# Selective scan: unit pairs of neighbouring channels, one 512 KB replication per pair, and another order of the y sums

## What is computed

```
xs = jnp.stack([x0, x1, x0[..., ::-1], x1[..., ::-1]], axis=1)        # 4 directions k
delta = jax.nn.softplus(dts + dt_projs_bias[None, :, :, None])
def step(h, inp):
    u_t, d_t, B_t, C_t = inp
    h = jnp.exp(d_t[..., None] * A) * h + (d_t * u_t)[..., None] * B_t[:, :, None, :]
    y = jnp.einsum('bkdn,bkn->bkd', h, C_t)
    return (h, y)
ym = ys[:, 0:2] + ys[:, 2:4][..., ::-1]
y = ym[:, 0] + ym[:, 1].reshape(B, D, W, H).transpose(0, 1, 3, 2).reshape(B, D, L)
```

## Time and profile before

| | |
|---|---|
| runs (3) | median 5447.71 us, 5444.3 to 5461.19 us |
| profiled execution, its own time | 5458.66 us |
| its span, first to last instruction | 5456.5 us |
| the scan's part of it | about 2756 to 5366 us |
| busy in the span: PE, DVE, ACT, POOL | 4633.9, 4354.1, 3138.7, 4137.1 us |

### The profile page before, as it was taken

The page is one execution under the profiler, slowest core; times in us unless marked ns, Lnnn a source line. Parts: engine busy times, 40 slices in busy tenths (PEclk is TensorE's granted clock), DMA queues, the critical chain, the costliest instruction groups (busy, mean ns, idle before and its releaser), DMA issues. The chain is left out here.

```text
span 5456.5 us, 68516 instructions
## 1 busy us (share of the span) xinstructions
PE 4633.9 (85%) x15210; PEld 2099.0 (38%) x15210; DVE 4354.1 (80%) x3524; ACT 3138.7 (58%) x6582; POOL 4137.1 (76%) x1958
## 2 busy tenths in 40 slices
PE   7998887956999999964978888888888888888887
PEld 2332554623666666642522222222222222222222
DVE  4776445452599999997969999999988999999995
ACT  6885555621111111101367788887878778888876
POOL 2454545532589898987869999899998999999993
PEclk9998999977999999977979999999998999999998
DMA  2000101067678787844067777777776777777773
GB/s 52 1 1 15 55 22 51 27 195 203 134 141 151 140 153 140 152 73 99 0 152 186 183 194 183 182 188 177 188 188 170 187 185 187 182 190 179 191 184 98
DMA packets 385380, 733.14 MB, mean 134 GB/s; under 512 B 77948, under 2 KB 119080, under 8 KB 370920
## 3 DMA queue, kind: packets, MB, share of 16 engines
q1 hardware_dynamic: 385128, 730.30, 56.8%
HBM read 594.31 MB, written 82.32 MB: 124 GB/s over the span
## 5 line engine op out<-in xcount | busy, mean ns | idle before, releaser
L2208 POOL TENSOR_TENSOR l_hc<-l_h,l_c_rep 128x1024 f32<-128x1024 f32 x768 | 1805.8, 2364 | 212.3 <-DVE l_h L2279 206.0
L1400 POOL TENSOR_TENSOR l2b_prod<-l2b_v,l2b_attn 128x1568 f32<-128x1568 f32 x276 | 937.9, 3458 | 232.0 <-ACT l2b_attn L1361 117.3
L2279 DVE TENSOR_TENSOR_SCAN l_h<-l_p,l_h,l_bu 128x1024 f32<-128x1024 f32 x448 | 1030.9, 2337 | 71.8 <-ACT l_bu L2116 70.7
L1964 PE MATMUL l_p<-l_stacked,l_pick 96*128 96x512 f32 x1536 | 656.2, 509 | 302.1 <-DVE l_h L2279 301.6
L2263 DVE TENSOR_TENSOR l_bu<-l_du_rep,l_p 128x1024 f32<-128x1024 f32 x512 | 616.5, 1204 | 133.9 <-DMA l_du_rep<-du_scratch 125.1
L1448 DVE TENSOR_REDUCE l2b_osum<-l2b_prod 128x32 f32<-128x1568 f32 x384 | 665.7, 1780 | 63.3 <-POOL l2b_prod L1400 59.5
L2197 POOL TENSOR_TENSOR l_pool_bu<-l_du_rep,l_b_sb 128x1024 f32<-128x1024 f32 x256 | 605.2, 2364 | 40.3 <-DMA l_du_rep<-du_scratch 40.3
L1964 PEld LDWEIGHTS l_p<-l_stacked,l_pick 96*128 96x128 f32 x1536 | 253.1, 196 | 989.2 <-DVE l_h L2279 815.1
L1973 PE MATMUL l_p<-l_hc,l_y_pick 128*32 128x512 f32 x3072 | 582.3, 646 | 3.7 <-POOL l_hc L2208 3.7
L1353 ACT ACTIVATE l2b_logits<-l2b_conv,l2b_this_b 98x512 f32<-98x512 f32 x96 | 66.2, 689 | 861.0 <-PE l2b_conv L1318 861.0
L2279 DVE TENSOR_TENSOR_SCAN l_h<-l_p,l_h,l_pool_bu 128x1024 f32<-128x1024 f32 x224 | 524.7, 2343 | 3.8 <-ACT l_pool_bu L2116 3.5
(11 more groups left out here) (269 smaller groups left out, 9066.2 us busy)
## 6 DMA issues: line engine op xcount, KB each, us to landing
l_du_rep<-du_scratch SPq DMA_DIRECT2D x1536, 256.0 KB, 5.2
l2b_img_high<-qkv_scratch SPq DMA_DIRECT2D x192, 306.2 KB, 5.7
l2b_img_low<-qkv_scratch SPq DMA_DIRECT2D x192, 306.2 KB, 9.5
l_stacked<-l_parts SPq DMA_DIRECT2D x512, 96.0 KB, 2.3
l2b_v<-v_scratch SPq DMA_DIRECT2D x192, 152.0 KB, 6.4
qkv_scratch<-l2a_strip SPq DMA_DIRECT2D x32, 840.0 KB, 5.2
du_scratch<-l_du SPq DMA_DIRECT2D x128, 192.0 KB, 2.1
l_w_raw<-L_w_sed SPq DMA_DIRECT2D x32, 576.0 KB, 3.7
```

Source lines behind the costliest of these rows:

```text
L1400: return eng.tensor_tensor(dst.rearrange("q x (dy dx) -> q x dy dx", dx=WIN), window, attn_half[:, :, unit % 2].rearrange("q x (dy dx) -> ...
L1964: pe.matmul(p_da[p % 2][:, e, :], pick[:, GRP[i] % (Q // DL), :], stacked[:, par, GRP[i] * DL // Q, :], start=True, stop=True).then_inc(s_ ...
L2208: pool.tensor_tensor(hc[:, slot:slot + 2, :], h[:, 2 * p:2 * p + 2, :], c_rep[:, par, :].unsqueeze(1).to_broadcast([128, 2, N]), ALU.mult) ...
L2279: dve.tensor_tensor_scan(flat(h[:, 2 * p:2 * p + 2, :]), flat(p_da[p % 2]), flat(of), state, ALU.mult, ALU.add).then_inc(s_h, 1)
```

## The change

A unit is now one channel parity: of 16 neighbouring channels the even ones are one unit and the odd ones the other, and the two make a pair. Two neighbouring rows of `du_scratch` lie behind each other in DRAM, so the du of a partition's two units is one run of 4 KB, where it was two runs of 2 KB. Each pair is replicated by one DMA of 512 KB where there were two of 256 KB, the ring has four slots of a pair in place of eight of a unit, and each product waits for one semaphore in place of two. SP replicates pair 0 of the next step right after the store of du, ahead of `restack`.

The y sums change their sets: the three units of a triple come from three pairs (the even units of pairs 0 to 2, then the odd ones, the same for pairs 3 to 5), where they were three units in a row. On PE the third triple and the fourth stand together ahead of the third pair's `replicate`; `low_mm` moves ahead of the fourth pair's `replicate`; `c_mm` moves behind the second triple. On ACT `turn_x` moves ahead of `low`. The constants `pick`, `y_pick` and `a_logs` are permuted to fit. DVE and POOL keep their order.

```diff
-    RING = 8
+    RING = 4
-    GRP = [(i % YT) * YJ + i // YT for i in range(G)]
+    GRP = [2 * (SETS * (p % YT) + p // YT) + e for p in range(PAIRS) for e in range(2)]
-        du_rep = sb("l3_du_rep", [128, RING, N])
+        du_rep = sb("l3_du_rep", [128, RING, 2, N])
...
-                src = du_d[par, GRP[i] * DL:(GRP[i] + 1) * DL]
-                src = bass.AP(src.tensor, src.offset, [[0, S], [N, DL], [1, N]])
-                sp_.dma_start(du_rep[:, ring_at(par, i)], src).then_inc(s_dur[ring_at(par, i)], 16)
+                first = GRP[2 * p] // 2 * (2 * DL)
+                src = du_d[par, first:first + 2 * DL]
+                src = bass.AP(src.tensor, src.offset, [[0, S], [2 * N, DL], [1, 2 * N]])
+                sp_.dma_start(du_rep[:, ring_at(par, p)].rearrange("q e n -> q (e n)"), src).then_inc(s_dur[ring_at(par, p)], 16)
...
             def step(n, par, more):
-                for i in range(RING, G):
-                    replicate_du(n, par, i)
+                for p in range(RING, PAIRS):
+                    replicate_du(n, par, p)
                 if more:
                     store_du(n + 1, 1 - par)
+                    replicate_du(n + 1, 1 - par, 0)
                     sp_.wait_ge(s_rep, G * n)
                     sp_.nop(nofuse=True)
                     restack(n + 1, 1 - par)
-                    for i in range(RING):
-                        replicate_du(n + 1, 1 - par, i)
+                    for p in range(1, RING):
+                        replicate_du(n + 1, 1 - par, p)
...
             def y_triple(n, t, par):
-                pe.wait_ge(s_hc, PAIRS * n + LAST_PAIR[t] + 1 + HC0)
+                first, e = YT * (t // 2), t % 2
+                pe.wait_ge(s_hc, PAIRS * n + first + YT + HC0)
...
-                                   hc[:, hc_at(par, i // 2) + i % 2, :], start=(t == 0), stop=False)
+                                   hc[:, hc_at(par, first + q) + e, :], start=(t == 0), stop=False)
...
                 if before:
                     y_triple(n - 1, 2, 1 - par)
+                    y_triple(n - 1, 3, 1 - par)
                 replicate(n, k, 2, par)
                 if before:
-                    y_triple(n - 1, 3, 1 - par)
                     y_whole(n - 1, *before)
+                if n1:
+                    low_mm(n + 1)
                 replicate(n, k, 3, par)
                 if n1:
-                    low_mm(n + 1)
                     b_mm(n + 1, 1 - par, *n1)
...
                 y_triple(n, 0, par)
                 replicate(n, k, 5, par)
+                y_triple(n, 1, par)
                 if n1:
                     c_mm(n + 1, *n1, n2)
-                y_triple(n, 1, par)
...
-                if n1:
-                    low(n + 1)
-                decays(n, k, c, 3)
-                if n1:
-                    b_copy(n + 1, 1 - par)
                 if k == 0:
                     if not isinstance(c, int):
                         turn_x(b, c + 2)
...
+                if n1:
+                    low(n + 1)
+                decays(n, k, c, 3)
+                if n1:
+                    b_copy(n + 1, 1 - par)
                 decays(n, k, c, 4)
...
-                triple = (2 * (freed % PAIRS) + 1) // YT
+                triple = 2 * (freed % PAIRS // YT) + 1
```

More of the change, by code:

```diff
@@ L1710, in selective_scan @@
     TRIPLES = G // YT
-    LAST_PAIR = [(YT * t + YT - 1) // 2 for t in range(TRIPLES)]
+    SETS = PAIRS // YT
     HCP = 4
-    RING = 8
+    RING = 4
     POOL_PAIRS = (2, 5)
@@ L1824, in all_steps, with ring_at, ring_count @@
             return run
[L1826 to L1832, removed]
+        def ring_at(par, p):
+            return (PAIRS * par + p) % RING
+        def ring_count(n, par, p):
+            return 16 * (2 * PAIRS // RING * (n - par) // 2 + (PAIRS * par + p) // RING) + 16
         def hc_at(par, p):
@@ L1876, in store_du, with replicate_du @@
                 sp_.dma_start(du_d[par], du[:]).then_inc(s_dus, 16)
-            def replicate_du(n, par, i):
-                if i == 0:
+            def replicate_du(n, par, p):
+                if p == 0:
                     sp_.wait_ge(s_dus, 16 * (n + 1) + DUS0)
                     sp_.nop(nofuse=True)
-                user, step_of = (i - RING) % G // 2, (i - RING) // G
+                user, step_of = (p - RING) % PAIRS, (p - RING) // PAIRS
                 if user in POOL_PAIRS:
@@ L1900, in step @@
                     restack(n + 1, 1 - par)
-                    for i in range(RING):
-                        replicate_du(n + 1, 1 - par, i)
+                    for p in range(1, RING):
+                        replicate_du(n + 1, 1 - par, p)
             store_du(0, 0)
+            replicate_du(0, 0, 0)
             restack(0, 0)
-            for i in range(RING):
-                replicate_du(0, 0, i)
+            for p in range(1, RING):
+                replicate_du(0, 0, p)
             step(0, 0, True)
@@ L1971, in y_triple @@
                 for q in range(YT):
-                    i = YT * t + q
                     mm = pe.matmul(p_y[q * 32:(q + 1) * 32, :], y_pick[:, t, :],
-                                   hc[:, hc_at(par, i // 2) + i % 2, :], start=(t == 0), stop=False)
+                                   hc[:, hc_at(par, first + q) + e, :], start=(t == 0), stop=False)
                 mm.then_inc(s_ymm, 1)
@@ L2189, in times_b @@
                     pool.nop(nofuse=True)
-                for e in range(2):
-                    pool.wait_ge(s_dur[ring_at(par, 2 * p + e)], ring_count(n, par, 2 * p + e))
-                    pool.nop(nofuse=True)
+                pool.wait_ge(s_dur[ring_at(par, p)], ring_count(n, par, p))
+                pool.nop(nofuse=True)
                 before = POOL_PAIRS[at - 1] + 1 if at else POOL_PAIRS[-1] + 1 - PAIRS
@@ L2195, in times_b @@
                     pool.wait_ge(s_h, PAIRS * n + before + H0)
-                slot = ring_at(par, 2 * p)
-                pool.tensor_tensor(pool_bu[:], du_rep[:, slot:slot + 2, :], b_sb[:, par, :].unsqueeze(1).to_broadcast([128, 2, N]),
+                pool.tensor_tensor(pool_bu[:], du_rep[:, ring_at(par, p)], b_sb[:, par, :].unsqueeze(1).to_broadcast([128, 2, N]),
                                    ALU.mult).then_inc(s_pbu, 1)
@@ L2250, in delta_u @@
                 dve.tensor_tensor(du[:], p_bc[0:C, :], u_of(b, k, c), ALU.mult).then_inc(s_du, 1)
-            def loaded(n, i, par):
-                dve.wait_ge(s_dur[ring_at(par, i)], ring_count(n, par, i))
             def times_b(n, p, par):
-                slot, at = ring_at(par, 2 * p), DVE_PAIRS.index(p)
+                at = DVE_PAIRS.index(p)
                 used = DVE_PAIRS[at - 2] if at >= 2 else DVE_PAIRS[at + 2] - PAIRS
@@ L2260, in times_b @@
                 dve.wait_ge(s_bcp, n + 1)
-                loaded(n, 2 * p, par)
-                loaded(n, 2 * p + 1, par)
-                dve.tensor_tensor(bu[:, at % 2], du_rep[:, slot:slot + 2, :],
+                dve.wait_ge(s_dur[ring_at(par, p)], ring_count(n, par, p))
+                dve.tensor_tensor(bu[:, at % 2], du_rep[:, ring_at(par, p)],
                                   p_b[par].unsqueeze(1).to_broadcast([128, 2, N]), ALU.mult).then_inc(s_bu, 1)
@@ L2426, in selective_scan_layout @@
         for dl in range(DL):
-            pick[:, j * DL + dl, j, :, dl] = 1
+            pick[:, j // 2 * 2 * DL + 2 * dl + j % 2, j, :, dl] = 1
     y_pick = np.zeros((S, DL, 4, 4 * DL), np.float32)
@@ L2430, in selective_scan_layout @@
         for dl in range(DL):
-            y_pick[:, dl, grp, grp * DL + dl] = 1
+            y_pick[:, dl, grp, grp // 2 * 2 * DL + 2 * dl + grp % 2] = 1
     return {
@@ L2438, in selective_scan_layout @@
         "ident": np.eye(C, dtype=np.float32),
-        "a_logs": g["A_logs"].reshape(K, G, DL, S).transpose(3, 2, 0, 1).reshape(S * DL, K * G),
+        "a_logs": g["A_logs"].reshape(K, G // 2, DL, 2, S).transpose(4, 2, 0, 1, 3).reshape(S * DL, K * G),
         "cols": np.concatenate([g["dt_projs_bias"].T, g["Ds"].reshape(K, C).T], 1),
```

## The result

The changed kernel takes 5300.18 us (median of 4 runs, 5295.29 to 5308.44), the kernel before beside it 5454.45. The ratio is 0.972, 95% interval 0.9696 to 0.9743. That is 154 us less, where the sum of the prediction had 110.

A forecast was written before the change was run, and what follows sets the result against it. DVE and POOL were taken as equal floors, 18.7 us a step, with only their waiting to win. -115 - 14 + 19 = -110 from the profiled 5458.66 gives 5348.7, 5338 us at the median; 8-in-10 range 5280 to 5395 us.

The forecast's parts named there:

- Pair 0 ahead of the stacking: On SP: replication issued once the du store lands, so DVE's wait for it goes except the longest; 115 us less.
- The stack behind it: The four stacking DMAs, now queued behind pair 0's replication, land later but before they are needed; costed at nothing.
- the rival of 5448: Stacking DMAs land some 5 us late, so the wait only moves to them; 5448 us, no gain; chance 0.08.
- the cover of 1.8 us: On PE: the stack may come as late as 4021.4, 1.8 us beyond its worse landing bound of 4019.6.
- Six DMAs for twelve: On SP: half the replications, same bytes, packets of 4 KB for two of 2 KB; no cost or gain.
- ACT and PE: Earlier `low_mm` and `turn_x` shorten direction 0's steps; bounds 0 and 28 us, half taken: 14 us less.
- Direction 0's excess: Sign of being right: the 7 us that direction 0 takes beyond direction 3 in eight steps halves.
- the wait of 0.38 before scan 3: In direction 3, `low` also waits for ACT to take y, so this 0.38 us wait shrinks little.
- The loop over the triples: Loop through POOL, PE, ACT and DVE by scan 2: 18.7 us, the same as DVE's and POOL's floors.
- the rival of 5397: The triples' loop exceeds its parts, DVE waits for ACT before scan 2, 64 us taken back; 5397 us, chance 0.21.
- New coupling: Three loops of the same 18.7 us delay each other, 0.15 us a step over 128 steps; 19 us more.
- The clock rival: PE's clock falls at the two triples of each step, 26 us more for the stage; 5474 us, chance 0.11.

The follow-up runs named there:

- e1: The changed kernel with SP issuing pair 0's replication behind the four stacking DMAs again; 5408.57 us.
- e2: The kernel before with only SP's order changed: pair 0's two 256 KB replications ahead of the stacking DMAs; 5333.57 us.
- e3: The changed kernel with each pair's DMA cut into two of 256 KB with runs of 2 KB on the same semaphore; 5283.84 us.
- e4: The changed kernel with ACT's `turn_x` back behind the copy of B; 5300.04 us.
- f3: The changed kernel with POOL's C product and DVE's B product of pair 4 both made for the first unit only; 5275.23 us.
- e9: The changed kernel with the old PE and ACT orders (`low_mm`, fourth triple, `c_mm`, `turn_x` all back); 5366.54 us.
- f1: The changed kernel with POOL's C product of pair 4 made for the first unit only; 5292.52 us.
- f2: The changed kernel with DVE's B product of pair 4 made for the first unit only; 5299.66 us.

## Why the prediction was right, and where it was not

- **Pair 0 ahead of the stacking, -115.** Right: 108 to 110 us by e1 and e2, and DVE's wait for the DMA fell by 125.1 - 24.0 = 101 (to 24.0, where under 20 had been named as the sign). The first replication is issued where it was said (3.24 us into the step for 3.4) and lands 5.4 us later, inside the bounds of 4.4 to 6.3 and not at the lower one that was taken; it still comes 0.9 us early.
- **The stack behind it, nothing.** Right in the main. It lands 4.2 us after its issue for 2.3, 1.9 more, near the worse bound of 2.1 that the sum allowed for. The Trainium skill's rule ("DMA: Bandwidth & Descriptors", "Queues, rings and completion order") is that each DMA engine takes the descriptors of its ring in order. The trace agrees, by the 1.9 us. The wait did not move to the stack, and the rival of 5448 is out; but the cover of 1.8 us, read from one step, is not there in all. PE waits for the stack 37 times, 32.8 us in all, one of the signs named for being wrong, and how much of that reaches DVE is not shown.
- **Six DMAs for twelve, nothing.** By e3 it rather costs something, up to 16 us, which is likely and not settled.
- **ACT and PE, -14.** The step that failed. `turn_x` was named as the cause and is worth nothing (e4). Direction 0's excess has not halved in the stretch shown (10.4 us for 7.0); where it is gone, in the last image, e4 has the same 152.32 us for direction 0 without the earlier `turn_x`. What was said of `low_mm`, "so that the wait of 0.38 before scan 3 shrinks little", is wrong: the wait is gone. The working looked at ACT's taking of y as what `low` waits for, and did not ask what the taking of y waits for, although shows its 1.61 us of wait for PE. It hangs on PE's order, and from the third triple to scan 3 the chain is 0.75 us shorter with the changed order (f3 against e2).
- **The loops.** The loop over the triples was added up through scan 2, 18.7 us. DVE waits for ACT before scans 2 and 5 (`l_pool_bu`) only 25 times, 8.0 us in all, so the rival of 5397 is out. The longer loop goes through `y_whole`, the taking of y, `low` and scan 3; in direction 3 it was 19.0 us in e2, above the floors, and with the changed order it is about 18.4 (f3). This loop was not among the steps at all. Its size over the whole scan is argued and not shown: with 0.3 us above the floors, 128 steps would make 38 us, and e2 and the change lie 33 apart (5333.57 and 5300.18), about what the forecast lacks. But in direction 2 the loop does not stand above the floors; DVE's wait for ACT's additions in e2, split by direction, is 31, 16, 2 and 16 us in directions 0 to 3. That the two numbers are so near is in part luck.
- **New coupling, +19.** Too much at first sight: steps of 18.56 us without a wait occur. But the layout with the old order costs 33 us (e9 against e2), so there is a cost of coupling. Most of what the traces show of it is in the ring of `hc` (POOL's 60.8 us in e9) rather than in the spread of waits; the larger DMAs may be part of it. `c_mm`'s move, which the sum left out, stands at that place.
- **The clock rival, 5474.** Out: 1.00 in direction 3 with two triples in a row.

So the forecast, 5338 us, was 38 too high: the term of the DMA was right to a few us, and -14 + 19 should have been about -40. That the result lies within the range all the same is owed to the width of the range, and for this part not to the working.

## What to carry to other kernels

When a DMA is ready long before its queue reaches it, look at what the queue waits for ahead of it; that order alone was 110 of 154 us here. After that, add up each loop through all the engines to the instruction that shows the wait, and ask of each piece what it waits for in turn: a small wait of 0.38 us was the visible end of a chain through PE, ACT and DVE. Do so for each kind of step: the chain was long in direction 3 and not in direction 2. Where two engines and a loop have the same length, cutting work from one of them gives nothing (f1, f2).

## What was not expected of the hardware

At the same 197 GB/s the DMA engines are busy 0.85 of the time with 512 KB transfers of 4 KB runs, and 0.75 with 256 KB transfers of 2 KB runs (the stretches of the change and of e3): the larger transfers with the longer runs cost more engine time here, not less. Which of the two does it was not separated; e2, with the old units in 256 KB transfers of 2 KB runs, has 0.79 at 196 GB/s in the same stretch. And with transfers of 64 partitions by this pattern the stretch runs at 124 GB/s, about half of the 246 of the earlier trace rows, and the kernel is 23% slower than the kernel before.
